# Last layer's sums: a step's sixteen weights go through TensorE into PSUM, and VectorE's product reads them there

## What is computed

```python
h = (x @ W).reshape(N, H, C)                       # H = 4, C = 32
e = leaky_relu(<h[row], a_i> + <h[col], a_j>, 0.2)  # one score an edge and head
e = where(mask_of_the_8_largest_of_the_row, e, -inf)
ez = exp(e - segment_max(e, row)[row])
alpha = ez / segment_sum(ez, row)[row]
out = segment_sum(alpha[:, :, None] * h[col], row)
return elu(out.reshape(N, H * C))
```

## Time and profile before

| what | value |
|---|---|
| time, median of 3 runs (lowest to highest) | 8679.93 us (8676.5 to 8685.21) |
| the profiled execution: its own time | 8693.18 us |
| its span, first to last instruction | 8691.1 us |
| mean granted TensorE clock | 0.772 of full |
| sums of the last layer in it | about 7456 to 8609 us |

### The profile page before, as it was taken

The page is one execution under the profiler, slowest core; times in us unless marked ns, Lnnn a source line. Parts: engine busy times, 40 slices in busy tenths (PEclk is TensorE's granted clock), DMA queues, the critical chain, the costliest instruction groups (busy, mean ns, idle before and its releaser), DMA issues. The chain is left out here.

```text
span 8691.1 us, 192168 instructions
## 1 busy us (share of the span) xinstructions
PE 5916.9 (68%) x40472; PEld 4854.3 (56%) x40473; DVE 6071.0 (70%) x12108; ACT 1746.5 (20%) x5063; POOL 6425.4 (74%) x7809
## 2 busy tenths in 40 slices
PE   6666666665788587777777549999588830566442
PEld 4455555553677466666666437777378720455332
DVE  5555555556777887777777448888599899898335
ACT  1111111111211444444444102222500010111000
POOL 6777777776788377777777778887277778877774
PEclk6555555555899799999999669999799965899555
DMA  6778888875477266666666669998189953798664
GB/s 198 218 216 219 219 217 220 218 219 168 130 210 211 70 212 205 207 206 206 207 206 207 211 196 268 273 270 239 35 245 263 260 145 87 197 255 237 163 163 110
DMA packets 1900193, 1739.84 MB, mean 200 GB/s; under 512 B 163065, under 2 KB 1624495, under 8 KB 1899807
## 3 DMA queue, kind: packets, MB, share of 16 engines
q1 hardware_dynamic: 1216980, 816.75, 32.2%
q10 hardware_dynamic: 496812, 471.17, 19.3%
q0 software_dynamic: 186160, 449.72, 18.5%
HBM read 1285.39 MB, written 452.43 MB: 200 GB/s over the span
## 5 line engine op out<-in xcount | busy, mean ns | idle before, releaser
L1877 POOL DMA_INDIRECT z_xg<-table,srci x1664 | 1781.6, 1071 | 512.7 <-issue 457.4
L1414 POOL DMA_INDIRECT sorted<-e_score,srci x1612 | 1628.2, 1010 | 602.8 <-issue 427.2
L461 POOL DMA_INDIRECT g_xg<-table,srci x1612 | 1553.9, 964 | 539.5 <-issue 470.0
L481 PE MATMUL g_psg<-g_wg,g_eT 128*128 128x136 f32 x3224 | 1027.5, 474 | 0.0
L1957 PE MATMUL z_ps<-z_wrow,z_oh 128*128 128x132 f32 x3712 | 652.1, 330 | 501.9 <-issue 332.6
L1735 PE MATMUL n_ps<-n_row,n_oh 128*128 128x257 f32 x3712 | 881.2, 389 | 93.2 <-DVE n_row L1711 79.3
L1957 PEld LDWEIGHTS z_ps<-z_wrow,z_oh 128*128 128x128 f32 x3712 | 559.4, 228 | 594.6 <-issue 557.3
L481 PEld LDWEIGHTS g_psg<-g_wg,g_eT 128*128 128x128 f32 x3224 | 769.3, 324 | 191.9 <-issue 191.9
L1735 PEld LDWEIGHTS n_ps<-n_row,n_oh 128*128 128x128 f32 x3712 | 677.7, 190 | 298.0 <-issue 216.4
L479 PE MATMUL g_psg<-g_bias,g_ones 3*128 3x272 bf16 x806 | 318.4, 395 | 675.6 <-DVE g_es L570 646.8
L1473 PE MATMUL m_psx<-acc,e_score 128*128 x3608 | 600.5, 317 | 197.8 <-DVE e_score L1598 122.9
(11 more groups left out here) (426 smaller groups left out, 12696.0 us busy)
## 6 DMA issues: line engine op xcount, KB each, us to landing
n_row<-sorted SPq DMA_DIRECT2D x464, 520.0 KB, 4.4
z_buf<-gathered ACTq DMA_DIRECT2D x464, 256.0 KB
g_keys<-dst_row ACTq DMA_DIRECT2D x451, 256.0 KB, 3.8
ag_buf<-gated SPq DMA_DIRECT2D x451, 256.0 KB, 3.3
m_keys<-dst_row ACTq DMA_DIRECT2D x451, 256.0 KB
gathered<-z_xg SPq DMA_DIRECT2D x416, 256.0 KB
gated<-g_y SPq DMA_DIRECT2D x403, 256.0 KB
g_eT<-in_attr_t SPq DMA_DIRECT2D x402, 256.0 KB
```

The costliest lines, as they stand in the source:

```text
L461: nc.gpsimd.indirect_dma_start(out=xg[:, u, j, :], out_offset=None, in_=v.table[:, :], in_offset=bass.IndirectOffsetOnAxis(ap=v.srci[:, t: ...
L481: last = nc.tensor.matmul(psg[u % 2][:, h, j * W:(j + 1) * W], eT[:, u % R, (h * H + j) * P:(h * H + j + 1) * P], wg[:, :], start=False, s ...
L1414: nc.gpsimd.indirect_dma_start(out=v.sorted[:, :], out_offset=bass.IndirectOffsetOnAxis(ap=place[:, t:t + 1], axis=0), in_=rows[:, u, j, : ...
L1877: nc.gpsimd.indirect_dma_start(out=xg[:, u, j, :], out_offset=None, in_=v.table[:, :], in_offset=bass.IndirectOffsetOnAxis(ap=v.dsti[:, t: ...
```

## The change

In each step TensorE multiplies the identity with the 16 weights of the step's group, so that they stand in PSUM bank 3, in one of its two places by turns. VectorE's product reads the weights there and no longer in `e`; it has one more wait, for that product (`s_wt`). The new function `weigh` runs on TensorE one step ahead of `sums`, with a register load for the group's number, and waits until VectorE is done with the place it writes. ScalarE's copy of the weights into `wrow` still reads `e`. TensorE waits before its loop until ScalarE has put all weights into `e`.

```diff
@@ stage_last_layer
+    s_wt = sem("z_weight")
...
+        weight = bank[3][:, :, 0:G * H]
...
                     last.then_inc(s_mm, 1)
 
-                pipeline(pe, KS, (sums, 0), ring=R)
+                def weigh(k, u, use):
+                    g = step_value(nc, pe, steps, 0, k, GS - 1)
+                    if later(k, 2):
+                        pe.wait_ge(s_w, k - 1)
+                    nc.tensor.matmul(weight[:, u % 2, :], v.ident[:, :], flat(e[:, ds(g * G, G), 0:H]), start=True,
+                                     stop=True).then_inc(s_wt, 1)
+
+                pe.wait_ge(s_bc, H * KR)
+                pipeline(pe, KS, (weigh, 0), (sums, 1), ring=R)
...
                     dve.wait_ge(s_ld[u], use * 16 + 16)
+                    dve.wait_ge(s_wt, k + 1)
                     nc.vector.tensor_tensor(
                         wrow[:, u, :, 0:C].rearrange("p t (h c) -> p t h c", h=H),
                         buf[:, u, :, :].rearrange("p t (h c) -> p t h c", h=H),
-                        e[:, ds(g * G, G), 0:H][:, :, :, None].broadcast_to([P, G, H, C // H]),
+                        weight[:, u % 2, :].rearrange("p (t h) -> p t h", h=H)[:, :, :, None].broadcast_to([P, G, H, C // H]),
                         ALU.mult).then_inc(s_w, 1)
```

## The result

The changed kernel takes 8605.69 us (median of 4 runs, 8601.62 to 8608.0) against 8678.48 us before (4 runs): a ratio of 0.9911, interval 0.99 to 0.9923. Forecast were 8603 us, which is 0.9911 of the 8679.93 us that were known then. The profiled execution took 8608.0 us, with a span of 8606.0 us.

A forecast was written before the change was run, and what follows sets the result against it. GpSimd's gathers were taken to bound the end of the sums, with TensorE's and VectorE's added work hidden. 8679.93 us less 77 us of gather prolongation gave 8603 us, 8 in 10 within 8590 to 8640 us.

The forecast's parts named there:

- The bound: While the sums run: GpSimd, issuing 847 gathers from 7460 us on, sets their end; the last addition follows 13.2 us later.
- the first stretch: Sums from 7460 to 7985 us, using groups gathered earlier, 1.66 us a step; after the change to last some 590 us.
- What the change takes away: Gathers beside the sums: prolongation under VectorE's product with two SBUF sources goes, 77 us of a possible 0 to 78.
- The reading that I built on the box: VectorE's f32 product: only two-port modes block GpSimd's descriptors, so gain 0; weighed as a rival, no change having 0.05.
- The costs: Sums' steps: VectorE's product +10 ns, perhaps +0.05 us a step with its wait; `weigh` 0.3 us on TensorE, hidden.
- rival (a): Gathers and loads beside the sums: DMA takes part back, gain 30 to 60 us, 8620 to 8650 us; chance 0.07.
- Rival (c): TensorE in the sums: clock stays at 1.2 GHz, 2.9 us a step, some 190 us longer, 8870 us; chance 0.04.

The follow-up runs named there:

- 2: Changed kernel with both PSUM places filled once before the loop, no identity product or wait per step: ratio 0.9912 to the kernel before, 8610.29 us.
- 9: Changed kernel with the identity product made two times a step: ratio 0.9907 to the kernel before, 8612.87 us.
- 10: Changed kernel with two more identity products of 128 columns a step, results unread: ratio 0.991 to the kernel before, 8612.82 us.
- 8: Changed kernel with two more VectorE copies a step, 128 floats each from PSUM to SBUF: ratio 0.9915 to the kernel before, 8611.4 us.
- 1: Changed kernel, but VectorE's product reads the weights in `e` (SBUF) again; TensorE's product and both waits stay: ratio 0.9983 to the kernel before, 8673.77 us.
- 3: Changed kernel, but the one-hot instruction reads its count from `iota`, so it has two SBUF sources: ratio 0.9997 to the kernel before, 8680.82 us.
- 7: Changed kernel with two more VectorE copies a step, 440 floats each from SBUF to SBUF: ratio 0.9992 to the kernel before, 8680.45 us.
- 5: Changed kernel with the identity product made three times a step: ratio 1.0313 to the kernel before, 8961.98 us.
- 4: Kernel before, with the one-hot instruction's count read from SBUF, so both long instructions have two SBUF sources: ratio 1.0036, 8720.31 us.

## Why the prediction was right, and what in it was not

**The bound.** Right: GpSimd sets the end of the sums. Four kernels (the changed one, 2, 9 and 10) have steps between 1.64 and 1.73 us in the first stretch and all stand at 0.9907 to 0.9912, and 8, with 525 x 10/2781 = 1.89 us, stands at 0.9915. Every kernel that prolongs the gathers is slower, also with VectorE's and TensorE's work equal or nearly so (1 and 3).

**What the change takes away.** 77 us forecast, 77.5 us measured in the gathers. The cause, that a VectorE instruction with two SBUF sources holds a gather up, is shown from both sides: taken away for the product (the change), brought back for it (1), and brought in by another instruction (3). As a statement on which instructions do so it was too narrow (7). That the median came within 3 us of the forecast is in part luck: the runs of the two kernels spread over 6 and 9 us, and the two profiled executions are 85.2 us apart where the medians are 72.8.

The Trainium skill's "SBUF — State Buffer" has both halves: its section on the two sides of SBUF names VectorE operations with two SBUF inputs, against a GpSimd operation that reads SBUF, and operations in a two-port mode. 1 and 3 bear the first out. 7 agrees with the second as far as the copy's speed tells its mode, which the trace doesn't show. The reading that I built on the box in the same section of that page of the Trainium skill, which names only the two-port mode, would have given no gain, and it fell.

**The costs.** VectorE's product was to take 10 ns longer; it took 676 ns in place of 681. The Trainium skill's "VectorE: DVE Perf Modes", in its table of corrected cycles in the section on the errata, has 120 fixed cycles with a source in PSUM and 58 with one in SBUF, by my estimate from its 0.96 GHz 65 ns more an instruction; this trace doesn't show them for a product with one source in each. The `weigh` product was put at 0.3 us in TensorE's gap; most in the changed kernel's timeline take 0.29 us, and 2 shows that it costs 0.03 us a step and nothing at the end. DMA: I worked out 269 GB/s for the first stretch, and it is 268 at a share of 0.98; rival (a), a brake from there, didn't come, for the gathers' spacing stayed at 1.25 us. The first stretch was to last 590 us; the DMA share falls from 0.91 (7960 to 8060 us) to 0.64 (8060 to 8160 us), so it ends near 8050 us, as said.

**Rival (c)** didn't come, but my reason against it was poor and its price too high. I said that the clock would not stay low since TensorE "gets more work, not less". Three products a step are more work still, and there the clock stays at 0.50 with TensorE busy all the time (5). Between one product and three lies one that still runs at 0.99 (9). The change was two products away from being a loss of 3%, which nothing in my argument shows. The price was 2.9 us for a step with one product at the low clock; it is 2.17 us. The ten records follow each other without the gap of 0.3 us, and take 0.22 us each in such a row, not the 0.26 us of eight records that stand alone. By that, 464 x 2.17 = 1007 us is less than the 1059 us of the gathers, so even a clock that stayed low would hardly have moved the end of the sums with one product; that is an estimate, as no run held it low with one. The 273 us that 5 takes more than the kernel before look like (c)'s 190 us, but they come from a step with three products.

## What to carry to other kernels

Where GpSimd issues indirect DMAs and is what others wait for, compare the mean duration of one with its minimum; if they differ, lay the long ones beside VectorE's instructions. One source moved to PSUM freed them here for 0.3 us of idle TensorE a step, and didn't slow VectorE. Two such instructions a step cost less than twice as much as one (859 x (1074 - 945) ns = 111 us in 4 against 78 us before), so here removing the first of two brought less (36 us) than removing the last (73 us). Gathers that fall into step with VectorE are a likely reason. And a TensorE product of few columns put into a loop should be looked at by the granted clock after, not by the gap it fills.

## What the runs showed of the hardware that I hadn't expected

- TensorE at the low clock with no idle time: 895 us of busy time in 895 us at 0.50 (three products of 16 columns beside four of 132 a step), and 0.99 with two of them, or with one and two of 128 columns. The clock was low in all of them when the sums began.
- VectorE's f32 copy from SBUF to SBUF, with a single source, prolongs gathers (mean 1024 ns), and a copy from PSUM doesn't (944 ns).
- Gathers locked to VectorE's step in parts of the first stretch: median 1152 ns with one such instruction and 1162 ns with two, each with its 0.305 us about the 1.46 us of a step.
